# Thresholded spikes and a feed-forward table: another way to the idle row, other homes for sums, and another order of the loads

## The chip, the cores and the metric

One core of one Trainium2 chip. The metric is the device time of one execution of the kernel in microseconds (us); lower is better.

## The reference

`x` is (2, 2048, 512) float32, `cond` (2, 512), `w1` (512, 2048), `w2` (2048, 512). Cut to what matters:

```python
def _L0_cond_ref(inputs, initial_state):
    rates = jax.nn.relu(inputs) * DT                       # DT = 0.001
    c = initial_state[:, None, :] + jnp.cumsum(rates, axis=1)
    fl = jnp.floor(c)
    prev = jnp.concatenate([jnp.floor(initial_state)[:, None, :], fl[:, :-1, :]], axis=1)
    return (fl - prev) / DT

def _L0_ffn_ref(x, w1, b1, w2, b2):
    h = jax.nn.relu(jnp.einsum('bsd,dw->bsw', x, w1) + b1)
    return jnp.einsum('bsw,wd->bsd', h, w2) + b2

out = x + _L0_ffn_ref(_L0_cond_ref(x, cond), w1, b1, w2, b2)
```

Along the 2048 tokens each of the 2 x 512 channels passes a whole number very rarely, so nearly every row of spikes is zero. A token without a spike (an idle one) gets `x + relu(b1) @ w2 + b2`, the same row for all. A token with one spike in channel d gets the idle row and, on top, row d of a table `(relu(w1[d] / DT + b1) - relu(b1)) @ w2`. A token with more spikes goes through the network itself.

## The kernel before

All is float32. `x` is cut into 128 blocks of 16 tokens, a block to a partition, so that a batch is one tile `x_sb[b]` of 128 x 16 x 512. The inner width 2048 is cut into 16 chunks `m` of 128. Each engine has a list of work written out by hand, and semaphores tie the lists together.

**Loads** are issued by SyncE (SP) in one row (L272 to L297). `w_pairs` holds for each chunk the 128 rows of w1 transposed and of w2 side by side, 512 KB; a piece of `x` is two tokens of every block, 512 KB, eight to a batch (`load_x`). Pairs and pieces alternate. Then come `b2` and `w1` in four parts (L297, 4 MB in all, for the network's first layer), and last the stores of the finished idle rows (`store_idle`, L299), each behind a wait.

**ScalarE** makes each chunk of w1 into what the table needs by two steps, L422 and L423 (`table_chunk`), and copies the running sums out of PSUM (`copy_sums`, L427) behind chunks 6 and 11.

**TensorE** starts with eight products of ones (L900), and then multiplies chunk after chunk into four PSUM banks `ps_table` (L807): four products of 512 columns a chunk, each two records of the profile. Between the chunks stand small products that VectorE waits for or feeds (L901 to L931): `sum_totals(b)` makes block totals into running sums over blocks (L844), `spread_tokens(b)` writes the found tokens into all partitions (L856), `count_leads` (L862) and `find_slots` (L879) number the tokens with several spikes. Behind the table come the network's first layer (L888) and second layer (L895) for those tokens.

**VectorE** sums each batch over the 16 tokens of a block (`block_totals`, L547 to L552), so that `find_blocks` (L559 to L563) can tell in which block a channel passes its threshold; it then lists the blocks. **GpSimd** gathers the 16 values of each channel in its block (L342, four gathers a batch), and `find_tokens` (L582 to L588) finds the token in the block. `count_met` (L600), `find_leads`, `find_slots`, `first_spikes` and `second_spikes` prepare the rows of the network. Small levels and names are made early (`rise_levels`, `names`, L516 to L539).

**The idle row.** VectorE adds nine chunks of `relu(b1) * w2` into `idle_part` in SBUF (`idle_by_hand`, L509). TensorE adds the other seven and the part in four strips of 32 partitions (`add_strips`, L823 and L827), ScalarE copies them (L446), one product joins them (`join_strips`, L833), and ScalarE copies the row to SBUF (L448). It also stays in the bank `ps_idle`. Then it is added to all of `x_sb`: VectorE adds four tokens at once, with the row from PSUM (`add_idle`, L673, five times), GpSimd one token at once with the row from SBUF (L354, twelve times). GpSimd's additions wait for the semaphore `reading_psum` (L359 to L363), which VectorE raises ahead of steps of its own that read PSUM (L597, L706, L714).

At the end GpSimd adds the table's rows to the output by indirect DMAs (L347), behind the stores of the idle rows, and writes the rows of the network (L381).

Of the kernel before, what the change touches and what calls it, by code (L numbers as in the profile page):

```python
# [13 lines left out]
P = 128  # L14
# [4 lines left out]
def spike_ffn(nc, x, x_turned, cond, cond_cols, w1, w_pairs, b1_cols, b2, out):  # L19

# [14 lines left out]
    STRIP = 32  # L38
    STRIPS = P // STRIP
    BY_HAND = 9  # L40
# [14 lines left out]
    with ExitStack() as ctx:  # L55
# [6 lines left out]
        def psum(name):  # L62
            return ctx.enter_context(nc.psum_tensor(name, [P, 512], F32))

        x_sb = [sb(f"x_sb{b}", [P, BLK, D]) for b in range(B)]
        w_sb = sb("w_sb", [P, FC, 2, D])
        w1_sb = sb("w1_sb", [P, DC, F])
        total_two = [sb(f"total_two{b}", [P, TH, D]) for b in range(B)]
# [4 lines left out]
        idle_base = sb("idle_base", [P, D])  # L73
# [26 lines left out]
        strip_i = sb("strip_i", [P, 1], I32)  # L100
        strip_first = sb("strip_first", [P, 1])
# [38 lines left out]
        table_hidden = w_sb[:, :, 0, :]  # L140
        w2_sb = w_sb[:, :, 1, :]
        hidden = [w_sb[:, m // 4, 0, m % 4 * P:(m % 4 + 1) * P] for m in range(FC)]
        table_row = [w_sb[:, 4 + c, 0, :] for c in range(DC)]
        new_row = w_sb[:, 8, 0, :]
# [20 lines left out]
        ps_met = psum("ps_met")  # L165
        ps_small = psum("ps_small")
# [9 lines left out]
        w_in = [sem(f"w_in{m}") for m in range(FC)]  # L176
        w2_first_in = sem("w2_first_in")
# [4 lines left out]
        const_ready = sem("const_ready")  # L182
        ones_ready = sem("ones_ready")
# [33 lines left out]
        strip_first_ready = sem("strip_first_ready")  # L217
        strips_summed = sem("strips_summed")
        strips_copied = sem("strips_copied")
        idle_summed = sem("idle_summed")  # L220
        idle_copied = sem("idle_copied")
        reading_psum = sem("reading_psum")
# [32 lines left out]

        def redo_count(eng):

            return eng.value_load(redo_i[0:1, 0:1], min_val=1, max_val=BLK + 1)  # L258
# [4 lines left out]
        def _(sp):  # L263
            def load_pair(m):
                sp.dma_start(w_sb[:, m, :, :], w_pairs[m * P:(m + 1) * P, :, :]).then_inc(w_in[m], 16)
# [6 lines left out]
            sp.dma_start(w_sb[:, 0, 0, :], w_pairs[0:P, 0, :]).then_inc(w_in[0], 16)  # L272
            sp.dma_start(w_sb[:, 0, 1, :], w_pairs[0:P, 1, :]).then_inc(w2_first_in, 16)
            load_pair(1)
            sp.dma_start(start_c[:, :], cond_cols).then_inc(start_in, 16)
            load_x(0)
            load_pair(2)
            load_x(1)
            for m in range(3, 8):
# [713 lines left out]
```

## Time and profile before

| what | us |
|---|---|
| three runs | 104.23, 104.07, 102.87 |
| median | 104.07 |
| span of the profiled execution, first to last instruction | 102.1 |
| TensorE busy in it | 95.4 |
| VectorE | 65.9 |
| ScalarE | 35.5 |
| GpSimd | 43.2 |

The profile's page gives the span of the profiled execution and not its time with what lies around the span; the median of the runs is 1.97 above the span. Engines are named PE (TensorE), PEld (its weight loads), DVE (VectorE), ACT (ScalarE), POOL (GpSimd) and SP (SyncE) in the rows. L12 is line 12 of the kernel. A record of an engine's step gives its start from the span's begin and its length; in square brackets stands how long the engine sat idle before it, and what ended that.

### The profile page before, as it was taken

How to read it: one execution, taken by the hardware profiler on the slowest of the kernel's cores; microseconds unless marked ns; L12 is line 12 of the kernel's file. 1: busy time of each engine (PE TensorE's matmuls, PEld its weight loads, DVE VectorE, ACT ScalarE, POOL GpSimd, SP SyncE). 2: the span in 40 equal slices, each digit the busy share in tenths (PEclk: the TensorE clock that was granted, in tenths of full speed). 3: DMA queues.
4: the chain of work that ended last, by engine and by line, in shares of the span. 5: the costliest groups of instructions: out<-in, count | busy, mean ns of one | idle time of the engine just before them, and what ended most of it. 6: DMA issues, size and time to landing. Idle time of an engine off the chain costs nothing.

```text
span 102.1 us, 1157 instructions
## 1 busy us (share of the span) xinstructions
PE 95.4 (93%) x370; PEld 54.0 (53%) x370; DVE 65.9 (64%) x142; ACT 35.5 (35%) x64; POOL 43.2 (42%) x44
## 2 busy tenths in 40 slices
PE   5999999999999999999969999999999999999910
PEld 5944444444644444644234564649999984444300
DVE  2448999888699999488958888899993020020020
ACT  2796515315372540569740000003953330000000
POOL 6350000000078700017508181499937883688040
PEclk9999999999999999999999999999999999999996
DMA  1999999999999999999999725427999999998701
GB/s 58 286 387 414 417 420 411 411 407 409 409 409 409 396 393 401 409 394 387 379 373 352 324 116 218 193 125 292 395 430 436 407 336 195 218 115 106 92 8 62
DMA packets 10028, 31.66 MB, mean 310 GB/s; under 512 B 1671, under 2 KB 1799, under 8 KB 8994
## 3 DMA queue, kind: packets, MB, share of 16 engines
q1 hardware_dynamic: 8304, 29.63, 74.7%
q0 software_dynamic: 1568, 1.90, 11.4%
q8 instruction: 5, 0.08, 0.3%
q14 instruction: 5, 0.04, 0.1%
q10 hardware_dynamic: 146, 0.01, 0.1%
HBM read 21.58 MB, written 10.75 MB: 316 GB/s over the span
## 4 chain that ended last, share of the span: by engine, by line
PE 50%; DVE 20%; POOL 13%; issue 11%; ACT 1%; POOLq 1%; DVEq 0%
PE ps_table L807 40%; DVE x_sb L673 11%; POOL out L347 11%; PE ps_small L900 4%; DVE same L600 3%; PE ps_idle L823 2%; PE ps_turn L844 2%; DVE hot L619 1%; PE ps_idle L827 1%; PE ps_idle L833 1%; DVE spk_t L634 1%; POOL out L381 1%; POOL general_x L370 1%; POOLq L258 1%; DVE spk_t L629 1%
## 5 line engine op out<-in xcount | busy, mean ns | idle before, releaser
L807 PE MATMUL ps_table<-w_sb 128*128 128x512 f32 x128 | 56.9, 595 | 0.0
L807 PEld LDWEIGHTS ps_table<-w_sb 128*128 128x128 f32 x128 | 23.6, 190 | 27.1 <-issue 26.4
L342 POOL DMA_INDIRECT rates<-in_x_turned,sixteen_at x8 | 9.9, 1236 | 33.9 <-DVE sixteen_at L563 32.1
L354 POOL TENSOR_TENSOR x_sb<-x_sb,idle_row 128x512 f32<-128x512 f32 x12 | 14.9, 1277 | 9.9 <-DVEq L706 3.7
L422 ACT ACTIVATE w_sb<-w_sb,b_col 128x512 f32<-128x512 f32 (+2 forms) x19 | 12.2, 643 | 16.5 <-DMA w_sb<-in_w_pairs 16.3
L549 DVE SCALAR_TENSOR_TENSOR total_two<-x_sb,total_two 128x1024 f32<-128x1024 f32 x14 | 17.1, 1225 | 1.2 <-DMA x_sb<-in_x 0.8
L347 POOL DMA_INDIRECT out<-w_sb,to_single x8 | 12.5, 1558 | 5.8 <-issue 3.7
L895 PE MATMUL ps_table<-w_sb 128*128 128x512 f32 x32 | 14.0, 595 | 0.0
L423 ACT ACTIVATE w_sb<-w_sb,minus_relu_b 128x512 f32<-128x512 f32 (+2 forms) x19 | 12.3, 649 | 0.6
L673 DVE TENSOR_TENSOR x_sb<-x_sb,ps_idle 128x2048 f32<-128x2048 f32 x5 | 11.2, 2283 | 1.5 <-ACT idle_row L448 1.3
L895 PEld LDWEIGHTS ps_table<-w_sb 128*128 128x128 f32 x32 | 6.0, 190 | 7.2 <-issue 6.9
L452 ACT ACTIVATE w_sb<-ps_turn,b_col 128x128 f32<-128x128 f32 x8 | 2.9, 367 | 19.0 <-PE ps_turn L888 18.4
L888 PE MATMUL ps_small<-spk_t,w_sb 128*128 128x128 f32 x64 | 8.5, 275 | 0.0
L888 PE MATMUL ps_turn<-spk_t,w_sb 128*128 128x128 f32 x64 | 8.5, 275 | 0.0
L888 PEld LDWEIGHTS ps_turn<-spk_t,w_sb 128*128 128x128 f32 x64 | 7.9, 192 | 0.5 <-DVE spk_t L634 0.3
L888 PEld LDWEIGHTS ps_small<-spk_t,w_sb 128*128 128x128 f32 x64 | 7.8, 192 | 0.0
L509 DVE SCALAR_TENSOR_TENSOR idle_part<-w_sb,relu_b,idle_part 128x512 f32<-128x512 f32 x9 | 6.7, 750 | 1.5 <-DMA w_sb<-in_w_pairs 1.4
L729 DVE TENSOR_TENSOR w_sb<-ps_table,general_x 128x512 f32<-128x512 f32 x1 | 0.7, 692 | 6.3 <-PE ps_table L895 6.3
L900 PE MATMUL ps_small<-ones 128*128 128x128 f32 x16 | 3.7, 427 | 1.1 <-POOLq L320 1.1
L727 DVE TENSOR_TENSOR general_x<-general_x,b_row 128x512 f32<-128x512 f32 x1 | 0.7, 691 | 6.2 <-DMA general_x<-in_x,from_general 6.2
L900 PEld LDWEIGHTS ps_small<-ones 128*128 128x128 f32 x16 | 3.5, 330 | 1.1 <-POOLq L320 1.1
L665 DVE TENSOR_SCALAR crowd<-ps_table 128x1 f32<-128x1 f32 x1 | 0.2, 159 | 6.1 <-PE ps_table L871 6.1
(113 smaller groups left out, 65.5 us busy)
## 6 DMA issues: line engine op xcount, KB each, us to landing
x_sb<-in_x SPq DMA_DIRECT2D x16, 512.0 KB, 14.3
out<-x_sb SPq DMA_DIRECT2D x8, 1024.0 KB, 4.1
w_sb<-in_w_pairs SPq DMA_DIRECT2D x15, 512.0 KB, 15.7
w_sb<-in_w SPq DMA_DIRECT2D x4, 1024.0 KB, 15.3
w_sb<-in_w_pairs SPq DMA_DIRECT2D x2, 256.0 KB, 2.9
b_row<-in_b SPq DMA_DIRECT2D x1, 256.0 KB, 15.3
rates<-in_x_turned,sixteen_at POOLq DMA_INDIRECT x8, 6.5
out<-w_sb,to_single POOLq DMA_INDIRECT x8
```

The lines of the kernel that those rows point to most:

```text
L342: pool.indirect_dma_start(out=rates[:, col, :], out_offset=None, in_=x_sixteen, in_offset=bass.IndirectOffsetOnAxis(ap=sixteen_at[:, col:c ...
L347: pool.indirect_dma_start(out=out_rows, out_offset=bass.IndirectOffsetOnAxis(ap=to, axis=0), in_=row, in_offset=None, bounds_check=last_ro ...
L354: last = pool.tensor_tensor(x_sb[b][:, t, :], x_sb[b][:, t, :], idle_row[:, :], ALU.add)
L422: chain(act.activation(weights, weights, ACT.Relu, bias=b1_col[:, m:m + 1], scale=PER_DT))
L423: act.activation(weights, weights, ACT.Identity, bias=minus_relu_b1[:, m:m + 1]).then_inc(table_hidden_ready, 1)
L509: step = dve.scalar_tensor_tensor(out=idle_part[:, :], in0=w2_sb[:, m, :], scalar=relu_b1[:, m:m + 1], in1=idle_part[:, :], op0=ALU.mult, ...
L549: chain(dve.scalar_tensor_tensor(out=total_two[b][:, :, :], in0=tokens, scalar=0.0, in1=total_two[b][:, :, :], op0=ALU.max, op1=ALU.add))
L673: last = dve.tensor_tensor(tokens, tokens, along(ps_idle[:, :], end - begin), ALU.add)
L807: last = pe.matmul(ps_table[c][:, :], table_hidden[:, m, c * P:(c + 1) * P], w2_sb[:, m, :], start=(m == 0), stop=(m == FC - 1))
L888: last = pe.matmul(ps_hidden[m % 2][:, 0:P], w1_sb[:, c, m * P:(m + 1) * P], spk_t[:, c, :], start=(c == 0), stop=(c == DC - 1))
L895: last = pe.matmul(ps_out[:, :], hidden[m], w2_sb[:, m, :], start=(m == 0), stop=(m == FC - 1))
L900: pe.matmul(ps_small[:, 0:P], ones[:, :], ones[:, :], start=True, stop=True)
```

## The change

- The idle row: VectorE adds all 16 chunks, with the running sum in the PSUM bank `ps_idle` instead of SBUF; the last step writes `idle_part` in SBUF. TensorE sums it over the partitions by one product with ones (`sum_idle`) behind chunk 7. Strips, joining and their copy are gone.
- The block totals run in two PSUM banks (`ps_total`, which `ps_met` and `ps_small` are now parts of) instead of SBUF; the last step of a batch writes SBUF. The first of them waits for the products of ones.
- `rise_levels` and `names` move from VectorE to GpSimd, with `copy_predicated` written as products and sums.
- GpSimd's queue: gathers of batch 0, twelve tokens of the idle row, gathers of batch 1, eight more tokens. `reading_psum` is gone; instead each addition waits until VectorE has summed the piece. VectorE adds three quarters instead of five.
- `w_pairs` is split: w1's chunks in a layout of their own (2 KB a partition), w2 in eight groups of one to three chunks. The order of the loads is new; `w1` stands in between the first stores.
- Orders on VectorE and TensorE are new.

The core of the diff:

```diff
 @block.sync
+            load_w1_turned(0)
+            load_w2(0)
+            load_w1_turned(1)
+            load_w2(1)
+            sp.dma_start(start_c[:, :], cond_cols).then_inc(start_in, 16)
+            load_w2(2)
+            load_w1_turned(2)
+            load_x(0)
+            load_x(1)
+            load_w1_turned(3)
+            load_x(2)
+            load_x(3)
+            load_w2(3)
+            load_x(4)
+            load_w1_turned(4)
+            load_x(5)
+            load_x(6)
+            load_w1_turned(5)
+            load_x(7)
+            load_w2(4)
+            load_w2(5)
+            load_w1_turned(6)
+            load_w2(6)
+            load_w2(7)
+            load_x(8)
+            load_w1_turned(7)
+            for h in range(9, 11):
+                load_x(h)
+            load_w1_turned(8)
+            for h in range(11, 14):
+                load_x(h)
+            load_w1_turned(9)
+            load_x(14)
+            load_x(15)
+            for m in range(10, FC):
+                load_w1_turned(m)
+            sp.dma_start(b2_row[:, :], b2.rearrange("(o d) -> o d", o=1).to_broadcast([P, D])).then_inc(b2_in, 16)
+            store_idle(0, 0)
+            store_idle(0, 1)
+            load_w1(0)
+            load_w1(1)
+            store_idle(0, 2)
+            load_w1(2)
+            load_w1(3)
+            store_idle(0, 3)
+            for q in (0, 3, 1, 2):
+                store_idle(1, q)
...
+    W2_GROUPS = ((0, 1), (1, 2), (2, 4), (4, 6), (6, 9), (9, 12), (12, 14), (14, 16))
+        ps_total = psum("ps_total", TH)
+        ps_met = ps_total[:, 0:512]
+        ps_small = ps_total[:, 512:1024]
...
 @block.gpsimd
+            def rise_levels():
+                pool.wait_ge(goals_ready, 1)
+                pool.wait_ge(start_in, 16)
...
+            rise_levels()
+            names()
+            pool.sem_inc(levels_ready, 1)
...
                 for t in range(begin, end):
+                    pool.wait_ge(x_summed[b], t // TH + 1)
                     last = pool.tensor_tensor(x_sb[b][:, t, :], x_sb[b][:, t, :], idle_row[:, :], ALU.add)
...
+            get_sixteens(0)
             pool.wait_ge(idle_copied, 1)
-            pool.wait_ge(reading_psum, 1)
-            add_idle(0, 12, 14)
-            pool.wait_ge(reading_psum, 2)
-            add_idle(0, 14, 16)
-            pool.wait_ge(reading_psum, 3)
-            add_idle(1, 12, 16)
-            add_idle(1, 8, 12)
+            add_idle(0, 0, 12)
+            get_sixteens(1)
+            add_idle(0, 12, 16)
+            add_idle(1, 0, 4)
...
 @block.scalar
+                if m == 8:
+                    act.wait_ge(idle_summed, 1)
+                    act.activation(idle_row[:, :], ps_idle[:, :], ACT.Copy).then_inc(idle_copied, 1)
...
 @block.vector
+                step = dve.scalar_tensor_tensor(out=ps_idle[:, :] if m < FC - 1 else idle_part[:, :],
+                                                in0=w2_sb[:, m, :], scalar=relu_b1[:, m:m + 1],
+                                                in1=ps_idle[:, :] if m > 0 else idle_part[:, :], op0=ALU.mult, op1=ALU.add)
...
+                    if h == 0:
+                        step = dve.tensor_scalar(sums, tokens, 0.0, None, ALU.max)
+                    else:
+                        step = dve.scalar_tensor_tensor(out=sums if h < XH - 1 else total_two[:, :, :], in0=tokens, scalar=0.0,
+                                                        in1=sums, op0=ALU.max, op1=ALU.add)
+                    step.then_inc(x_summed[b], 1)
+                    dve.wait_ge(x_summed[b], h + 1)
...
             first_columns()
+            for m in range(4):
+                idle_by_hand(m)
+            block_totals(0, 0, 4)
+            idle_by_hand(4)
+            idle_by_hand(5)
+            block_totals(0, 4, XH)
+            for m in range(6, 12):
+                idle_by_hand(m)
             find_blocks(0)
+            for m in range(12, FC):
+                idle_by_hand(m)
+            block_totals(1, 0, 2)
             find_bases(0)
+            block_totals(1, 2, XH)
             find_blocks(1)
             find_tokens(0)
             find_bases(1)
             count_met(0)
             find_leads(0)
+            add_idle(1, 12, 16)
             find_tokens(1)
             find_slots(0)
             count_met(1)
             find_leads(1)
             first_spikes()
             find_slots(1)
             second_spikes()
             add_idle(1, 4, 8)
+            add_idle(1, 8, 12)
...
 @block.tensor
+            for m in range(6, 8):
                 table_chunk(m)
+            sum_idle()
+            for m in range(8, 10):
+                table_chunk(m)
+            table_part(10, 0, 2)
             sum_totals(1)
+            table_part(10, 2, DC)
+            table_part(11, 0, 3)
             spread_tokens(0)
+            table_part(11, 3, DC)
+            table_part(12, 0, 3)
             count_leads(0)
             table_part(12, 3, DC)
+            table_part(13, 0, 2)
             spread_tokens(1)
+            table_part(13, 2, DC)
             find_slots(0)
```

## Rows read from the trace of the kernel before

**Rows 1.** The page, part 1: busy us of each engine, share of span, instructions

```profile
PE 95.4 (93%) x370; PEld 54.0 (53%) x370; DVE 65.9 (64%) x142; ACT 35.5 (35%) x64; POOL 43.2 (42%) x44
```

**Rows 2.** Timeline of TensorE: start us, us, engine, line, operation, out<-in, count

```profile
1.11 3.71 PE L900 MATMUL ps_small<-ones 128*128 128x128 f32 x16 [1.11 <-POOLq L320]
4.66 20.79 PE L807 MATMUL ps_table<-w_sb 128*128 128x512 f32 x48
...
48.21 1.49 PE L823 MATMUL ps_idle<-w_sb,relu_b 128*32 128x512 f32 x11
...
52.95 1.88 PE L807 MATMUL ps_table<-w_sb 128*128 128x512 f32 x4
...
58.33 0.60 PE L856 MATMUL ps_turn<-ident,token 128*128 128x128 f32 x4
...
68.93 1.05 PE L888 MATMUL ps_turn<-spk_t,w_sb 128*128 128x128 f32 x8
...
83.36 13.98 PE L895 MATMUL ps_table<-w_sb 128*128 128x512 f32 x32
```

**Rows 3.** Groups of VectorE, shapes apart: busy us, mean ns of one, idle before

```profile
L549 DVE SCALAR_TENSOR_TENSOR total_two<-x_sb,total_two 128x1024 f32<-128x1024 f32 x14 | 17.1, 1225 | 1.2 <-DMA x_sb<-in_x 0.8
...
L509 DVE SCALAR_TENSOR_TENSOR idle_part<-w_sb,relu_b,idle_part 128x512 f32<-128x512 f32 x9 | 6.7, 750 | 1.5 <-DMA w_sb<-in_w_pairs 1.4
...
L600 DVE SCALAR_TENSOR_TENSOR same<-ps_met,token,weigh 128x512 bf16<-128x512 f32 x4 | 3.0, 751 | 0.1
...
L552 DVE TENSOR_TENSOR total<-total_two 128x512 f32<-128x512 f32 x2 | 1.4, 692 | 0.1
L559 DVE TENSOR_TENSOR under<-ps_turn,theta_sum 128x512 f32<-128x512 f32 x2 | 1.4, 692 | 2.3 <-PE ps_turn L844 2.3
...
L547 DVE TENSOR_SCALAR total_two<-x_sb 128x1024 f32<-128x1024 f32 x2 | 1.4, 690 | 0.4 <-DVE idle_part L509 0.4
```

**Rows 4.** Timeline of ScalarE: its steps on chunks 4, 6 and 11 as they land

```profile
15.59 0.72 ACT L422 ACTIVATE w_sb<-w_sb,b_col 128x512 f32<-128x512 f32 x1 [2.37 <-DMA w_sb<-in_w_pairs]
...
23.25 0.72 ACT L422 ACTIVATE w_sb<-w_sb,b_col 128x512 f32<-128x512 f32 x1 [2.35 <-DMA w_sb<-in_w_pairs]
24.01 0.72 ACT L423 ACTIVATE w_sb<-w_sb,minus_relu_b 128x512 f32<-128x512 f32 x1
...
41.04 0.72 ACT L422 ACTIVATE w_sb<-w_sb,b_col 128x512 f32<-128x512 f32 x1 [2.54 <-DMA w_sb<-in_w_pairs]
```

**Rows 5.** Timeline of VectorE

```profile
28.87 2.49 DVE L549 SCALAR_TENSOR_TENSOR total_two<-x_sb,total_two 128x1024 f32<-128x1024 f32 x2
...
41.26 0.69 DVE L552 TENSOR_TENSOR total<-total_two 128x512 f32<-128x512 f32 x1
...
56.10 0.42 DVE L582 TENSOR_SCALAR rates<-rates 128x64 f32<-128x64 f32 x1
...
65.15 2.29 DVE L673 TENSOR_TENSOR x_sb<-x_sb,ps_idle 128x2048 f32<-128x2048 f32 x1 [0.24 <-DVE hot L619]
```

**Rows 6.** Timeline of GpSimd: gathers of the rates, additions of the idle row

```profile
30.18 2.00 POOL L342 DMA_INDIRECT rates<-in_x_turned,sixteen_at  x1 [0.30 <-issue]
...
45.58 0.94 POOL L342 DMA_INDIRECT rates<-in_x_turned,sixteen_at  x1 [10.09 <-DVE sixteen_at L563]
...
53.96 2.51 POOL L354 TENSOR_TENSOR x_sb<-x_sb,idle_row 128x512 f32<-128x512 f32 x2 [3.69 <-DVEq L706]
...
65.14 9.93 POOL L354 TENSOR_TENSOR x_sb<-x_sb,idle_row 128x512 f32<-128x512 f32 x8 [3.44 <-DVEq L714]
```

**Rows 7.** The tile `rates`: ns min/median/max of a step, and the gathers' landing

```profile
L582 DVE TENSOR_SCALAR rates<-rates x2: 191/304/418, 45.2 to 56.1; 128x64 f32<-128x64 f32 x2
...
DMA to landing us min/median/max: 5.3/6.5/7.2
```

**Rows 8.** Windows: us, then each engine's busy us (instructions), clock, DMA share, GB/s

```profile
7.30:10.86 3.56, 3.56 (x10) 1.65 (x9) 2.98 (x19) 2.58 (x5) 0.00 (x0) 1.00 1.03 413
...
100.00:101.00 1.00, 0.00 (x0) 0.00 (x0) 0.00 (x0) 0.00 (x0) 0.00 (x0) 0.60 0.39 150
```

More of the change, by code:

```diff
@@ L16, with spike_ffn @@
 PER_DT = float(np.float32(1.0 / float(np.float32(DT))))
-def spike_ffn(nc, x, x_turned, cond, cond_cols, w1, w_pairs, b1_cols, b2, out):
+def spike_ffn(nc, x, x_turned, cond, cond_cols, w1, w1_turned, w2_rows, b1_cols, b2, out):
     B, S, D = x.shape
@@ L138, in spike_ffn @@
         redo_i = sb("redo_i", [P, 1], I32)
[L140 to L144, printed above, removed]
+        hidden = [table_hidden[:, m // 4, m % 4 * P:(m % 4 + 1) * P] for m in range(FC)]
+        table_row = [table_hidden[:, 4 + c, :] for c in range(DC)]
+        new_row = table_hidden[:, 8, :]
         again = x_sb[0]
@@ L175, in spike_ffn @@
         x_in = [[sem(f"x_in{b}_{h}") for h in range(XH)] for b in range(B)]
-        w_in = [sem(f"w_in{m}") for m in range(FC)]
-        w2_first_in = sem("w2_first_in")
+        w1_turned_in = [sem(f"w1_turned_in{m}") for m in range(FC)]
+        w2_in = [sem(f"w2_in{g}") for g in range(len(W2_GROUPS))]
         w1_in = [sem(f"w1_in{i}") for i in range(WQ)]
@@ L182, in spike_ffn @@
         const_ready = sem("const_ready")
+        goals_ready = sem("goals_ready")
+        levels_ready = sem("levels_ready")
+        warm_ended = sem("warm_ended")
+        x_summed = [sem(f"x_summed{b}") for b in range(B)]
         ones_ready = sem("ones_ready")
@@ L254, in own @@
             return slice(b * DC, (b + 1) * DC)
+        w2_group = [g for g, (begin, end) in enumerate(W2_GROUPS) for _ in range(begin, end)]
         def redo_count(eng):
@@ L336, in _, with names, get_sixteens @@
+            def names():
+                pool.wait_ge(const_ready, 3)
+                chain(pool.tensor_copy(slot_name[:, :], slot_i[:, :]))
+                chain(pool.tensor_copy(sixteen_f[:, :], sixteen_i[:, :]))
+            rise_levels()
+            names()
+            pool.sem_inc(levels_ready, 1)
             last_row = pool.to_reg(ROWS - 1)
-            for b in range(B):
+            def get_sixteens(b):
                 pool.wait_ge(sixteen_listed, b + 1)
@@ L899, in _ @@
             for _ in range(WARM):
-                pe.matmul(ps_small[:, 0:P], ones[:, :], ones[:, :], start=True, stop=True)
+                last = pe.matmul(ps_small[:, 0:P], ones[:, :], ones[:, :], start=True, stop=True)
+            last.then_inc(warm_ended, 1)
             for c in range(DC):
```

186 lines of the change are left out of this document (46 added, 140 removed).

## Prediction

> **What bounds the kernel now.** I read the page first: TensorE is busy in 95.4 of 102.1 us [rows 1]. Then TensorE's timeline, which shows the end being set by that row of work: eight products of ones from 1.1, the table from 4.7 in records of 0.43 us (20.79 us for 48; a product of two records is 0.86, a chunk of four products 3.44), the first layer from 68.93, the second layer to 97.34, and hardly a gap [rows 2]. One stretch of it is not table work: from 48.21 to 52.95 stand the idle row's strips and their joining, and one table product that the program puts between them (L917). Everything after 68.93 is 28.4 us of TensorE and then a fixed tail of 4.8, and the change leaves both alone. So the question is one date: when does the first layer start? It needs all of the table ahead of it on TensorE's queue, and in that queue stand nine waits on results of VectorE (two of totals, the idle part, two spreads, two counts of leads, two of slots). So I read next what feeds those waits: VectorE's groups [rows 3], ScalarE's dates for the chunks' arrival [rows 4], VectorE's timeline [rows 5], GpSimd's timeline and its gathers' landing [rows 6, 7], and two windows [rows 8].
>
> The page gives the execution's span, 102.1; the median of the three runs is 104.07, so some 2.0 us lie around the span. I add changes of the span to the median.
>
> **TensorE's own work.** Removed: 52.95 - 48.21 = 4.74, less the table product in it, 0.86: 3.9 us [rows 2]. Added: one product of 512 columns, 0.86. Net -3.0, if nothing waits. This is the gain on offer.
>
> **Loads.** Count the SP queue in units of 256 KB. Before, chunk 4's pair is unit 18 and ScalarE starts on it at 15.59 the moment it lands; chunk 6's is unit 30, at 23.25; chunk 11's unit 56, at 41.04 [rows 4]. That is 0.64 us a unit, and 1.1 us more behind GpSimd's first gathers. ScalarE takes two steps of 0.72 with small gaps, 1.5 us, from landing to ready [rows 4]. After: w1's chunk 4 is unit 21 (lands 17.5, ready 19.0), chunk 6 unit 35 (26.5, 28.0), chunk 7 unit 42 (31.0, 32.5), chunk 9 unit 54 (39.6, 41.1). TensorE wants them at 4.8 + 3.44 a chunk and 0.9 for the first totals: chunk 4 at 18.6, so it waits 0.4; chunk 6 at 26.8, waits 1.2; chunk 7 at 31.4, waits 1.0; the idle product ends at 36.8; chunk 9 wanted at 40.2, waits 0.9. Sum 3.5 us, which is the gain given back. That w1 now comes in rows of 2 KB (pairs were 4 KB) no row prices apart; I take nothing, with 0 to 1 us by unit 54.
>
> **VectorE to the second totals.** It loses 3.5 us of small levels and names, 18 operations that fill the window from 7.30 to 10.86 [rows 8], and gains seven additions of 0.79 (0.75 and the gap, rows 3), 5.5 us. The first operation of each batch now writes PSUM. Its row is 0.69 for 1024 elements while the two-input form of the same size takes 1.23 [rows 3]; I take 1.23, since the fast rate is seen only between SBUF tiles, with 0.69 as the other bound (1.1 us for two). Other PSUM operands cost nothing: an addition from PSUM is 0.692 and one in SBUF 0.692 [rows 3]. The Trainium skill, VectorE: DVE Perf Modes, section on the TRN2 errata, gives an operation from PSUM 62 cycles of 0.96 GHz more than one from SBUF, some 0.06 us; an estimate by it is 2 us more over about 30 operations. By that page the second totals would be later still, but the two equal rows speak against it, and it stays out of the sum.
> Dates: x's eighth piece is unit 28, lands 22.0; totals end at 23.95, as before. Six idle additions to 28.65, the block search 1.7 (two steps of 0.69 like those of rows 3, a short one, gaps) to 30.3, four more to 33.4, two totals to 35.9, the bases 1.9 (two of 0.69, three short ones) to 37.8, six totals of 1.26 and the sum 0.69 to 46.1. Before it was 41.95 [rows 5]: 4.1 later, and VectorE, not the loads, sets it.
> Moved levels on GpSimd: some 25 chained small operations from 6.5. Between 0.3 and 0.9 us each they end at 14 to 29; they are wanted at 28.65. At 0.4 they are hidden.
>
> **GpSimd's queue, the step that decides.** Gathers of batch 0: with VectorE reading one SBUF tile only, four at 1.25 a piece, 30.6 to 35.6. Idle row copied at 36.9 + 0.6 = 37.5. Then twelve additions of 1.24 (9.93 for eight, rows 6) to 52.4, and only behind them the gathers of batch 1, which before were issued from 45.6 on. The last of four starts 3.75 us after the first, and lands 5.3 to 7.2 us after its issue [rows 7], I take 6: at best 52.4 + 3.75 + 6 = 62.2. Before, VectorE started on that batch's tokens at 56.10, held only by other work [rows 5].
>
> **What the two engines do to each other.** GpSimd's second gather takes 2.00 us instead of 0.94: it starts at 30.18 while VectorE adds two SBUF tiles until 31.36, and is 1.06 longer [rows 5, 6]. The other way: VectorE's rates step, 0.19 the other time, takes 0.42 from 56.10 [rows 5, 7] and ends at 56.52, right behind the end of GpSimd's additions at 56.47 [rows 6]. In no row does VectorE use two SBUF tiles while a further addition of GpSimd is queued; the steps beside GpSimd's eight additions from 65.14 read PSUM and keep their length. So the price of one such meeting lies between 0 and the rest of GpSimd's addition, 1.24. I take that rest, since both meetings that the trace has last to the end of the other's work. The Trainium skill, SBUF — State Buffer, section on who interferes with whom, calls the pair of interfaces that the two engines share an exclusive lock held for a whole instruction, which a VectorE instruction with one SBUF input doesn't need. By that rule the change is right to put its totals into PSUM and wrong to let the additions run beside the short steps between SBUF tiles: it gives rival A below, and its absence rival B.
> Short steps that now fall beside GpSimd's additions: the last of the bases at 37.7 (+1.2), the second total (+0.6, half an addition on average): totals at 47.9 instead of 46.1, so TensorE, which is there at 46.3 (chunk 9 from 41.1, then two products of chunk 10), waits 1.8. Then the second block search (+0.6), and three steps of batch 0's tokens until GpSimd is through, at about 54.1: token date 55.5 against TensorE's 53.3, wait 2.3. Bases 1.9, four counts of 0.8 [rows 3] and leads 0.6 end at 61.2: wait 1.8 at the first count of leads. VectorE adds its first quarter of the idle row, 2.3 [rows 5], to 63.5; the gathers, issued from 54.1, have landed at 63.9. GpSimd has begun eight more additions at 59.1, and ends them at about 70.2 with VectorE's steps between. Five steps of batch 1's tokens meet them, each 0.2 to 0.3 long and, but for the first, behind a whole addition: 63.9 + 0.6 + 4 x 1.45 makes 70.3, which is where the additions end, so 70.3 for the tokens. TensorE has been waiting since 63.9: 6.4 us.
> Behind that date TensorE has 11.4 us to the first layer: before, 10.6 from 58.33 [rows 2], and one table product more stands behind the spread now. VectorE's chain beside it, from the rates step to the last spikes, needs at most 68.93 - 56.10 less the idle addition of 2.3 that no longer stands in it [rows 2, 5], 10.5; it is covered. First layer at 81.7.
>
> **The clock.** TensorE's last product ends at 97.34 and it idles from there; the microsecond from 100 to 101 has a mean granted clock of 0.60, on the way from 2.4 GHz to the lower level of 1.2 [rows 8]. The first sixteen records ran at 0.23 us where equal ones at full rate take 0.11 [rows 2], so the stretch at the lower level cost 3.71 / 2 = 1.9 us. I take it that a wait of 6.4 us brings such a stretch once; bounds 0 and twice that. First layer at 83.5.
>
> **Sum.** 83.5 - 68.93 = +14.5; 104.07 + 14.5 = 118.5. GpSimd's rows to the output need about 20 us from the list at 87 and end before 107, while TensorE ends at 112: hidden, with 5 us of cover. w1, behind the early stores, is issued by 55 and lands by 65: wanted at 82, hidden by TensorE's wait.
>
> **Rivals.**
> *A, above*, 118.5, its own range 114.5 to 122. Chance 0.55.
> *B, late gathers alone.* VectorE's short steps are not held by GpSimd's additions, or hardly. Then tokens at 62.2 + 1.7 = 63.9, first layer at 75.3, and with the clock's 1.9 at 77.2: +8.3, 112.4; without the clock 110.5. For it: only one row shows a held VectorE step. 0.28.
> *C, GpSimd's additions hold the tile ports for the whole series.* They overlap (1.24 apart, 1.27 long, rows 6), so VectorE might not get in between. The bases' last step would wait from 37.7 to 52.4, and the second totals, 7.6 us of work, come at 60.8, which puts all behind it 6 us or more later than in A: 124 or more. Against it: GpSimd got in between VectorE's back-to-back steps at 31.36. 0.11.
> *D, the other side.* The early additions are short enough that batch 1's gathers are not late. It decides at VectorE's second block list, about 47.5: twelve additions in the 10.0 us from 37.5, 0.83 each where rows 6 show 1.24. Then TensorE's -3.0 stands. With the waits for loads as counted (3.5) it is 104.6; if the loads land some 1.2 us sooner than counted, which takes all four waits, it is 101.1. 0.06, half of it faster.
> The change may also not do what it says: were the totals in PSUM to hold GpSimd all the same, its additions get longer, which is A with a worse number.
>
> **How the numbers follow.** Predicted is A's 118.5. The range goes from B with no clock loss, 110.5, to A's upper end, 122.5; it leaves out C, D and the low edge of B, some 0.2. Faster by over 2% (what a measurement here can tell): 0.03; within 2%: 0.03; slower by over 2%: A, B, C, 0.94.
>
> **What would show it.** Right: TensorE's chain with waits for chunks 4, 6, 7 and 9 of 0.4 to 1.2 us; second totals 4 to 6 us later than 41.95; gathers of batch 1 issued from 52 to 55; the token steps beside GpSimd's additions at 1.2 to 1.5 us instead of 0.2; one wait of TensorE of 5 to 7 us ahead of the second spread, and a granted clock of half behind it; the first layer from 81 to 85. Wrong: token steps at their old 0.2 us (B), one VectorE step of over 5 us (C), the first layer ahead of 70 (D); and if the first operation into PSUM stays at 0.69, that term goes. The prediction fails as a whole if GpSimd's additions run well below 1.24 us.

## The result, and the profile after

Four executions of the changed kernel took 120.27 to 121.46 us, median 120.93, beside 104.15 for the kernel before on the same chip (102.87 to 104.32). The ratio is 1.166, with an interval of 1.157 to 1.175: slower by a sixth. 118.5 was predicted, with a range of 110.5 to 122.5. Ratios and times leave disturbed executions out (two of four of the first experiment, its profiled one among them, and one of four of the second).

The page of the profiled execution (120.95 us, span 119.1), its first part and the row of the granted clock in 40 slices:

```profile
PE 98.1 (82%) x354; PEld 54.7 (46%) x354; DVE 76.7 (64%) x129; ACT 34.8 (29%) x63; POOL 57.5 (48%) x77
...
PEclk9999999999999999999965555999999999999999
```

TensorE has 16 records fewer than in [rows 1] and is busy for 2.7 us longer: the stretch at 5 tenths of the clock adds some 3 us of busy time to work that got shorter, and the rest lies in short waits that the records cover. Where it stands still is in its timeline (start, length, line, count, and in brackets the idle time before and what ended it):

```profile
26.08 1.05 PE L842 MATMUL ps_turn<-up_to,total 128*128 128x128 f32 x8
28.07 3.70 PE L822 MATMUL ps_table<-w_sb,table_hidden 128*128 128x512 f32 x8 [0.93 <-ACT table_hidden L472]
32.58 3.70 PE L822 MATMUL ps_table<-w_sb,table_hidden 128*128 128x512 f32 x8 [0.82 <-ACT table_hidden L472]
36.12 1.02 PE L832 MATMUL ps_idle<-idle_part,ones 128*128 128x512 f32 x2
...
41.07 5.42 PE L822 MATMUL ps_table<-w_sb,table_hidden 128*128 128x512 f32 x12 [0.50 <-ACT table_hidden L472]
47.12 1.16 PE L842 MATMUL ps_turn<-up_to,total 128*128 128x128 f32 x8 [0.63 <-DVE total L582]
...
54.11 0.65 PE L854 MATMUL ps_total<-ident,token 128*128 128x128 f32 x4 [1.54 <-DVEq L621]
54.60 3.60 PE L822 MATMUL ps_table<-w_sb,table_hidden 128*128 128x512 f32 x8
68.69 0.59 PE L860 MATMUL ps_total<-leads_run,upper 128*128 128x1 f32 x2 [10.49 <-DVEq L641]
69.14 5.42 PE L822 MATMUL ps_table<-w_sb,table_hidden 128*128 128x512 f32 x6
74.40 0.60 PE L854 MATMUL ps_turn<-ident,token 128*128 128x128 f32 x4
...
85.65 1.05 PE L886 MATMUL ps_turn<-spk_t,w_sb 128*128 128x128 f32 x8
```

The strips are gone (one product at 36.12 in their place), five waits of 0.50 to 1.54 us have come in, and then one of 10.49 us ahead of the first count of leads. Behind it six records take 5.42 us where eight took 3.60 ahead of it. The first layer starts at 85.65 instead of 68.93 [rows 2]; from there to the second layer it is 14.4 us as before. So the whole loss, 16.7 us, again lies ahead of the first layer, and the longest wait is on VectorE. Its timeline there:

```profile
45.43 1.64 DVE L582 TENSOR_TENSOR total<-total_two 128x512 f32<-128x512 f32 x1
...
50.59 0.18 DVE L613 TENSOR_SCALAR rates<-rates 128x64 f32<-128x64 f32 x1
50.81 1.25 DVE L614 TENSOR_TENSOR_SCAN climb<-token_keep,rates 128x64 f32<-128x64 bf16 x1
52.09 1.13 DVE L616 TENSOR_TENSOR climb<-climb,sum_at 128x64 f32<-128x64 f32 x1
...
59.35 8.83 DVE L636 SCALAR_TENSOR_TENSOR is_first<-met,valid 128x4 f32<-128x4 f32 x1 [0.15 <-DVE same L629]
...
70.93 0.19 DVE L613 TENSOR_SCALAR rates<-rates 128x64 f32<-128x64 f32 x1
71.15 0.29 DVE L614 TENSOR_TENSOR_SCAN climb<-token_keep,rates 128x64 f32<-128x64 bf16 x1
71.48 0.23 DVE L616 TENSOR_TENSOR climb<-climb,sum_at 128x64 f32<-128x64 f32 x1
```

And GpSimd's:

```profile
37.86 15.28 POOL L405 TENSOR_TENSOR x_sb<-x_sb,idle_row 128x512 f32<-128x512 f32 x12 [2.12 <-ACT idle_row L494]
53.29 0.96 POOL L392 DMA_INDIRECT rates<-in_x_turned,sixteen_at  x1 [0.15 <-issue]
...
58.38 9.78 POOL L405 TENSOR_TENSOR x_sb<-x_sb,idle_row 128x512 f32<-128x512 f32 x8
```

Read the two together. Beside the first series (37.86 to 53.14) the steps of VectorE that take two SBUF tiles wait for the rest of an addition: 1.64 instead of 0.69, 0.73 instead of 0.16 (the list of blocks at 49.94), 1.25 instead of 0.29, 1.13 instead of 0.23. The step at 50.59, with one SBUF tile, keeps its 0.18 here; in other kernels such a step was held as well (last section). Beside the second series (58.38 to 68.16) a step over 4 columns, 0.16 us when free, takes 8.83 and ends 0.02 us behind the last addition: it was held not by one addition but by all that were left. The tokens of batch 1 then run at their free length.

The granted clock, in windows of one microsecond (us, busy time and instructions of the five engines, clock, DMA share, GB/s):

```profile
60.00:61.00 1.00, 0.00 (x0) 0.00 (x0) 1.00 (x1) 0.00 (x0) 1.00 (x2) 0.87 0.96 396
61.00:62.00 1.00, 0.00 (x0) 0.00 (x0) 1.00 (x1) 0.00 (x0) 1.00 (x1) 0.50 1.01 390
73.00:74.00 1.00, 1.00 (x2) 0.26 (x2) 0.52 (x1) 0.00 (x0) 0.00 (x0) 0.50 0.97 393
74.00:75.00 1.00, 1.00 (x6) 0.60 (x5) 0.00 (x0) 0.00 (x0) 0.00 (x0) 0.81 0.32 131
```

TensorE ran dry at about 58.2; in the microsecond from 60 the clock begins to leave 2.4 GHz, from 61 it is at 1.2, and it comes back within 74 to 75, more than 5 us after work was there again at 68.69.

### The profile page after: what moved, and what is told of

Same layout as the page of the kernel before. It is cut to its first block, busy times and chain, and to the rows that moved or that the text cites. A ratio compares the mean times of both kernels' runs of the same rounds, so it can differ in the third digit from the quotient of the medians.

```text
span 119.1 us, 1179 instructions
## 1 busy us (share of the span) xinstructions
PE 98.1 (82%) x354; PEld 54.7 (46%) x354; DVE 76.7 (64%) x129; ACT 34.8 (29%) x63; POOL 57.5 (48%) x77
## 4 chain that ended last, share of the span: by engine, by line
DVE 36%; PE 18%; issue 13%; POOL 11%; DMA 11%; SPq 7%; POOLq 1%; ACT 1%; DVEq 0%
PE ps_table L822 12%; DMA x_sb<-in_x 11%; POOL out L397 10%; DVE is_first L636 7%; DVE ps_total L577 6%; DVE ps_idle L558 6%; SPq L271 3%; DVE same L629 3%; SPq L258 2%; DVE total_two L577 2%; DVE total L582 2%; PE ps_turn L886 2%; PE ps_total L877 1%; SPq L262 1%; DVE under L602 1%
## 5 line engine op out<-in xcount | busy, mean ns | idle before, releaser
L822 PE MATMUL ps_table<-w_sb,table_hidden 128*128 128x512 f32 x128 | 60.8, 625 | 2.2 <-ACT table_hidden L472 2.2
L822 PEld LDWEIGHTS ps_table<-w_sb,table_hidden 128*128 128x128 f32 x128 | 24.5, 200 | 31.1 <-issue 24.7
L405 POOL TENSOR_TENSOR x_sb<-x_sb,idle_row 128x512 f32<-128x512 f32 x20 | 25.1, 1289 | 2.1 <-ACT idle_row L494 2.1
L397 POOL DMA_INDIRECT out<-table_hidden,to_single x8 | 12.5, 1559 | 23.5 <-ACT table_hidden L506 21.7
L471 ACT ACTIVATE table_hidden<-table_hidden,b_col 128x512 f32<-128x512 f32 (+2 forms) x19 | 12.2, 642 | 18.6 <-DMA table_hidden<-in_w_turned 18.6
L577 DVE SCALAR_TENSOR_TENSOR ps_total<-x_sb,ps_total 128x1024 f32<-128x1024 f32 x12 | 14.8, 1229 | 1.5 <-DMA x_sb<-in_x 1.1
L893 PE MATMUL ps_table<-w_sb,table_hidden 128*128 128x512 f32 x32 | 14.0, 595 | 0.0
L472 ACT ACTIVATE table_hidden<-table_hidden,minus_relu_b 128x512 f32<-128x512 f32 (+2 forms) x19 | 12.3, 649 | 0.6
L558 DVE SCALAR_TENSOR_TENSOR ps_idle<-w_sb,relu_b,ps_idle 128x512 f32<-128x512 f32 x14 | 10.6, 754 | 2.3 <-DMA w_sb<-in_w_rows 2.0
L893 PEld LDWEIGHTS ps_table<-w_sb,table_hidden 128*128 128x128 f32 x32 | 6.0, 190 | 7.2 <-issue 6.9
L636 DVE SCALAR_TENSOR_TENSOR is_first<-met,valid 128x4 f32<-128x4 f32 x2 | 9.0, 4496 | 0.3 <-DVE same L629 0.3
L886 PE MATMUL ps_total<-spk_t,w_sb 128*128 128x128 f32 x64 | 8.5, 275 | 0.0
## 6 DMA issues: line engine op xcount, KB each, us to landing
w_sb<-in_w_rows SPq DMA_DIRECT2D x2, 768.0 KB, 14.6
```

Source lines behind the costliest of these rows:

```text
L397: pool.indirect_dma_start(out=out_rows, out_offset=bass.IndirectOffsetOnAxis(ap=to, axis=0), in_=row, in_offset=None, bounds_check=last_ro ...
L405: last = pool.tensor_tensor(x_sb[b][:, t, :], x_sb[b][:, t, :], idle_row[:, :], ALU.add)
L471: chain(act.activation(weights, weights, ACT.Relu, bias=b1_col[:, m:m + 1], scale=PER_DT))
L472: act.activation(weights, weights, ACT.Identity, bias=minus_relu_b1[:, m:m + 1]).then_inc(table_hidden_ready, 1)
L558: step = dve.scalar_tensor_tensor(out=ps_idle[:, :] if m < FC - 1 else idle_part[:, :], in0=w2_sb[:, m, :], scalar=relu_b1[:, m:m + 1], in ...
L577: step = dve.scalar_tensor_tensor(out=sums if h < XH - 1 else total_two[:, :, :], in0=tokens, scalar=0.0, in1=sums, op0=ALU.max, op1=ALU.add)
```

## Experiments

Ratios are against the kernel before, run on the same chip. Eight kernels were run.

### The second series apart from the short steps, in two ways

What is open is why one step lasted 8.83 us, and what the time would be without it. The first kernel keeps GpSimd's second series back until the last spikes are made; the second lets it run at once, but puts a small step ahead of it that GpSimd waits for.

```diff
             get_sixteens(1)
+            pool.wait_ge(spikes_made, 1)
             add_idle(0, 12, 16)
...
             second_spikes()
+            dve.sem_inc(spikes_made, 1)
```

> The changed kernel with GpSimd's second series of eight additions held back until VectorE has made the last spikes; gathers and first series as they are. Theory S (VectorE's step between two SBUF tiles is held by the whole second series, 8.83 us, and TensorE's clock falls in that wait): the first leads come at about 60 instead of 68.6, the gathers of batch 1 land near 63.5 and then set the tokens at 65, the first layer starts at 76 to 78 instead of 85.65, no stretch at the half clock, and the time is 111 to 113 us. Theory N (the late gathers alone set the date, and the held step is hidden behind them): 120 to 121 us, no change.

```diff
             get_sixteens(1)
+            chain(pool.memset(joint[:, :], 0.0))
             add_idle(0, 12, 16)
```

> The changed kernel with one small memset on GpSimd, waited for to its end, between the gathers of batch 1 and the second series of eight additions. Theory K (the series holds its tile ports throughout because it follows the gathers without a wait, with GpSimd's cores out of step, so that no moment between two additions is free on all of them): VectorE's step of 8.83 us falls to at most 1.3, its later steps between SBUF tiles take 0.7 to 1.3 each while the series runs, and the time falls by 2 to 6 us, to 115 to 119. Theory L (whether a step gets in between two additions has nothing to do with what stands ahead of the series): the step stays at 8 to 9 us and the time at 120 to 121.

Held back: ratio 1.096 [1.088, 1.104], some 113.8 us, just above the 111 to 113 that were expected. Every VectorE step between the gathers and the held-back series has its free length (the scan 0.29, the addition behind it 0.23), and the step that took 8.83 takes 0.16. Its profiled execution differs from the expectation in two ways. The first layer starts at 78.60, not 76 to 78, and there is a stretch at the lower clock after all, of some 3.4 us, that begins in the microsecond from 66. Besides, the end is GpSimd's: its rows of batch 1 wait 7.22 us for a store of the idle rows, and the last row follows them without a gap at 109.53, while its value was ready at 107.81. So 113.8 us is not the price of the late gathers alone.

With the waited step: ratio 1.116 [1.109, 1.123], 116.0 us, inside what was expected. The series is as long as before, and the step over 4 columns has fallen from 8.83 us to 0.46. VectorE in this kernel:

```profile
59.86 0.46 DVE L638 SCALAR_TENSOR_TENSOR is_first<-met,valid 128x4 f32<-128x4 f32 x1 [0.15 <-DVE same L631]
60.36 1.18 DVE L640 SCALAR_TENSOR_TENSOR leads<-met,is_first 128x4 f32<-128x4 f32 x1
61.57 1.19 DVE L642 TENSOR_TENSOR_SCAN leads_run<-ones,leads 128x4 f32<-128x4 f32 x1
62.91 2.29 DVE L704 TENSOR_TENSOR x_sb<-x_sb,ps_idle 128x2048 f32<-128x2048 f32 x1
65.11 0.19 DVE L615 TENSOR_SCALAR rates<-rates 128x64 f32<-128x64 f32 x1
65.34 1.24 DVE L616 TENSOR_TENSOR_SCAN climb<-token_keep,rates 128x64 f32<-128x64 bf16 x1
66.61 1.13 DVE L618 TENSOR_TENSOR climb<-climb,sum_at 128x64 f32<-128x64 f32 x1
67.77 1.19 DVE L619 TENSOR_TENSOR under<-climb,theta 128x64 f32<-128x64 f32 x1
```

Behind the first, which meets only the rest of an addition, each step with two SBUF tiles lasts about one addition, 1.13 to 1.24. This is what the prediction had taken for both series.

### The same small step, not waited for

The waited step changes two things: there is an instruction between gathers and additions, and GpSimd stands still for a moment. The control leaves out the second.

```diff
             get_sixteens(1)
+            pool.memset(joint[:, :], 0.0)
             add_idle(0, 12, 16)
```

> Control for the joined kernel: the same small memset between the gathers and the second series, but nothing waits for it. Theory K (what frees the ports between additions is that all of GpSimd's cores start the series together): without the wait VectorE's step is again held for the whole series, 7 to 9 us, and the time is 119.5 to 122. Theory T (the memset only shifted the moment at which VectorE's step comes): the step stays at 0.5 to 1.3 us and the time at 115.5 to 117, as joined.

Ratio 1.167 [1.161, 1.172], the changed kernel's own. VectorE:

```profile
59.31 8.85 DVE L638 SCALAR_TENSOR_TENSOR is_first<-met,valid 128x4 f32<-128x4 f32 x1 [0.15 <-DVE same L631]
```

So the wait makes the difference and not the instruction. Nor is it the moment at which the step comes: it met the series 0.97, 0.96 and (totals in SBUF, below) 1.59 us behind its start where it was held throughout, and 0.82 us behind it where it was not. That a series started straight behind gathers keeps a VectorE step with two SBUF tiles out for its whole rest, and one started from a wait for one addition at a time, is shown; that GpSimd's cores run out of step in the first case is my picture of it, and no run here looks into it. Price: 120.9 - 116.0 = 4.9 us.

### GpSimd's additions let loose in the kernel before

```diff
             pool.wait_ge(idle_copied, 1)
-            pool.wait_ge(reading_psum, 1)
             add_idle(0, 12, 14)
-            pool.wait_ge(reading_psum, 2)
             add_idle(0, 14, 16)
-            pool.wait_ge(reading_psum, 3)
             add_idle(1, 12, 16)
```

> The kernel before, with the three waits of GpSimd's additions for VectorE's PSUM steps taken out: twelve additions in one series from about 53.8, as soon as the idle row is copied, with nothing else of the change. Theory S and K: the series starts behind a wait, so VectorE gets in between additions, each of its steps between SBUF tiles costs up to 1.25 us more until about 69, batch 1's tokens come 3 to 5 us later, and the time rises by 4 to 9 us, to 108 to 113. Theory L (a series can hold a step throughout at any time): one VectorE step of 6 us or more and a rise of over 9 us. Theory H (harmless, only the change's queue order matters): 103 to 105 us.

Ratio 1.058 [1.051, 1.065], 109.8 us, inside what was expected. The gathers are issued within 0.7 us of their dates before, nothing else is changed, and VectorE's steps show the price beside twelve additions that start from a wait:

```profile
55.72 0.28 DVE L579 TENSOR_SCALAR rates<-rates 128x64 f32<-128x64 f32 x1
56.03 1.29 DVE L580 TENSOR_TENSOR_SCAN climb<-token_keep,rates 128x64 f32<-128x64 bf16 x1
57.35 1.12 DVE L582 TENSOR_TENSOR climb<-climb,sum_at 128x64 f32<-128x64 f32 x1
...
62.10 1.72 DVE L616 TENSOR_TENSOR hot<-slot,slot_name 128x512 f32<-128x512 f32 x1
```

The first layer moves from 68.93 to 74.88. The three waits on `reading_psum`, which look like a loss of GpSimd's time, are worth 6 us.

### The totals back in SBUF

```diff
-    step = dve.tensor_scalar(sums, tokens, 0.0, None, ALU.max)
+    step = dve.tensor_scalar(total_two[:, :, :], tokens, 0.0, None, ALU.max)
...
-    step = dve.scalar_tensor_tensor(out=sums if h < XH - 1 else total_two[:, :, :], in0=tokens, scalar=0.0,
-                                    in1=sums, op0=ALU.max, op1=ALU.add)
+    step = dve.scalar_tensor_tensor(out=total_two[:, :, :], in0=tokens, scalar=0.0,
+                                    in1=total_two[:, :, :], op0=ALU.max, op1=ALU.add)
```

> The changed kernel with the block totals back in SBUF (both their first operations at 0.69 us instead of 1.23, so 1.1 us less of VectorE), everything else as changed. Theory S (two SBUF tiles collide with GpSimd's additions, PSUM totals don't): from about 37 on each of the last totals waits for an addition and each addition for a total; the second totals come at 51 to 54 instead of 47.1, GpSimd's first series ends at 58 to 62 instead of 53.1, and the time rises to 124 to 131 us. Theory P (the totals' home is worth nothing): 119 to 121, second totals 1 us earlier.

Ratio 1.214 [1.208, 1.220], 125.6 us, inside what was expected: the change's PSUM totals do what they are for. VectorE and, in the second fence, GpSimd:

```profile
37.44 12.26 DVE L577 SCALAR_TENSOR_TENSOR total_two<-x_sb,total_two 128x1024 f32<-128x1024 f32 x6
...
65.12 8.21 DVE L636 SCALAR_TENSOR_TENSOR is_first<-met,valid 128x4 f32<-128x4 f32 x1 [0.15 <-DVE same L629]
```

```profile
37.98 20.67 POOL L405 TENSOR_TENSOR x_sb<-x_sb,idle_row 128x512 f32<-128x512 f32 x12 [1.66 <-ACT idle_row L494]
```

Six operations take 2.04 us each instead of 1.23, and twelve additions 1.72 each instead of 1.27. With the totals in PSUM the same six take 6.29 (five) and 1.22 us, and only the joining step at the end (0.69 free, 1.64 here) is held.

### Gathers ahead of the additions, the second series kept back

```diff
             pool.wait_ge(idle_copied, 1)
-            add_idle(0, 0, 12)
+            add_idle(0, 0, 8)
             get_sixteens(1)
-            add_idle(0, 12, 16)
-            add_idle(1, 0, 4)
+            pool.wait_ge(spikes_made, 1)
+            add_idle(0, 8, 16)
...
             store_idle(0, 0)
             store_idle(0, 1)
             load_w1(0)
             load_w1(1)
-            store_idle(0, 2)
             load_w1(2)
             load_w1(3)
+            store_idle(0, 2)
...
             second_spikes()
+            dve.sem_inc(spikes_made, 1)
             add_idle(1, 4, 8)
+            add_idle(1, 0, 4)
```

> The changed kernel with only eight of GpSimd's additions ahead of the gathers of batch 1, the other eight of batch 0 behind VectorE's last spikes, and batch 1's first quarter added by VectorE; w1's last two parts are loaded ahead of the store of batch 0's third quarter. Theory S with late gathers: without the held step the gathers are the next limit (gate alone: 111 to 113), and 3.5 us earlier gathers bring the tokens to about 61.5, the first layer to 73 to 74.5 and the time to 108 to 110, where GpSimd's rows to the output begin to set the end. Theory G (behind the held step stands something other than the gathers, VectorE's own list or the loads): no more than 1 us below the gated kernel.

The first layer starts at 73.36, as expected, with no wait of TensorE above 1.2 us and no stretch at the lower clock. Even so it is 4.4 us later than before: in this trace the waits for chunks (4.2), second totals (0.9), leads (1.3) and tokens (1.1) outweigh the 3.0 saved. And the time is 112.5 (ratio 1.085 [1.079, 1.092]), above the expected 108 to 110: the end is no longer TensorE's. GpSimd at the end:

```profile
98.28 1.57 POOL L398 DMA_INDIRECT out<-table_hidden,to_single  x1 [3.97 <-DMA out<-x_sb]
...
105.69 1.03 POOL L431 DMA_INDIRECT out<-table_hidden,to_general  x1 [0.31 <-issue]
```

With the additions kept back until 71, the stores of the idle rows come late, the rows of batch 1 wait 3.97 us for them, and the last row follows them without a gap, while its value was ready at 102.6. So here the miss is that of the end, as in the kernel with the second series alone held back: I had priced GpSimd's queue only up to the first layer.

### Parts of the change on the kernel before

Levels and names on GpSimd, totals and idle sum in PSUM, 13 chunks and one round of strips instead of two, the second totals one product earlier on TensorE; everything else as before. The part of the diff that places the additions:

```diff
-    BY_HAND = 9
+    BY_HAND = 13
...
             find_bases(0)
             block_totals(1, 5, 6)
             idle_by_hand(8)
+            idle_by_hand(9)
+            idle_by_hand(10)
             block_totals(1, 6, XH)
+            idle_by_hand(11)
             find_blocks(1)
             find_tokens(0)
+            idle_by_hand(12)
```

> The kernel before with the parts of the change that cost nothing by the runs so far: levels on GpSimd, totals and the idle sum in PSUM, and with the freed time 13 chunks of the idle row by VectorE instead of nine, so four strips on TensorE instead of eight; the second totals one table product earlier; loads, GpSimd's queue and its waits for VectorE's PSUM steps as before. If TensorE's row sets the end and VectorE keeps up: 1 to 2 us below the kernel before, a ratio of 0.98 to 0.99. If VectorE's chain behind the gathers of batch 1 sets it (they land at 55 to 56 whatever the strips do): a ratio of 0.995 to 1.005. Over 1.01: the additions by hand have moved VectorE's chain late.

Ratio 1.019 [1.015, 1.023]: slower, though by how far it is from 2% can't be told; it is the third of the three expectations. TensorE, where the second totals are wanted:

```profile
43.93 1.16 PE L869 MATMUL ps_turn<-up_to,total 128*128 128x128 f32 x8 [1.76 <-DVE total L572]
```

The second totals end at 43.87 instead of 41.95: two additions more (1.6 us) and a first operation into PSUM (+0.54) stand ahead of them, with 0.24 of waiting for a load used up. And the 3.5 us that VectorE saved early bring nothing: batch 0's totals end at 24.2 here, 24.0 before and 24.1 in the changed kernel, because the landing of `x` sets them in all three.

The other try leaves levels and totals as they were, and puts the four additions more into waits that VectorE has:

```diff
-            find_blocks(0)
             idle_by_hand(6)
+            find_blocks(0)
...
-            block_totals(1, 6, XH)
+            block_totals(1, 6, 7)
+            idle_by_hand(9)
+            block_totals(1, 7, XH)
+            idle_by_hand(10)
+            idle_by_hand(11)
             find_blocks(1)
             find_tokens(0)
+            idle_by_hand(12)
...
-            add_idle(0, 4, 8)
             second_spikes()
+            add_idle(0, 4, 8)
...
-            table_part(12, 0, 1)
+            table_part(12, 0, 2)
             join_strips()
```

(and two more table products ahead of the second spread).

> The kernel before with one idea of the change (more of the idle row by hand) and new places for it. VectorE adds 13 chunks: the 7th stands in its wait ahead of the first block search, the 10th ahead of the last piece's totals, two in the 1.63 us wait behind the second totals, the last behind the tokens of batch 0. TensorE's strips then need one round of four instead of two (-0.9 us), two table products stand ahead of the joining instead of one (its wait of 0.8 us goes), two more ahead of the second spread, and VectorE's addition of 2.3 us moves from ahead of the last spikes to behind them. If TensorE's row and VectorE's chain behind the second spread bound the kernel before together, as its trace reads, both get shorter by some 1.5 us: first layer at 67.2 to 68.0 instead of 68.93, 102.4 to 103.2 us, ratio 0.983 to 0.992. If the additions by hand cost what they did in the kernel with levels on GpSimd, where the second totals came 1.9 us late, the ratio is 1.00 to 1.02.

Ratio 1.011 [1.007, 1.016]: no gain, and slightly slower, the second of the two expectations. TensorE does save 1.6 us, but the first layer starts at 68.78 against 68.93. The second totals came at 43.43, 1.5 later than before, behind a wait of 0.77 for a piece of `x` that the trace of before doesn't have at that place, and the second tokens at 58.78 instead of 57.81. At the end GpSimd waits 4.14 us for a store of the idle rows, instead of 2.06 (probably the moved addition made it later), and has 0.6 us left ahead of the last row instead of 3.8:

```profile
90.56 1.56 POOL L347 DMA_INDIRECT out<-w_sb,to_single  x1 [4.14 <-DMA out<-x_sb]
...
98.27 1.03 POOL L381 DMA_INDIRECT out<-w_sb,to_general  x1 [0.60 <-DVE w_sb L734]
```

The last row is issued 0.15 us earlier than before and lands 3.5 us later instead of 2.7, which makes up the 0.7 us by which this span is longer (102.8 to 102.1); why it lands later, no run shows. No version here beats the kernel before, where GpSimd has only those 3.8 us to spare ahead of the last row.

## Why the prediction was right, and where its steps were off

The sum by steps of TensorE, from start to start, so that filling and emptying count with the wait. "Due" is the start before plus 0.86 a product, 0.89 a totals step and 0.43 a spread (41.07 + 6 x 0.86 = 46.23, and so on; 24 products from 4.67 give 25.31):

| step | predicted | measured |
|---|---|---|
| strips gone, one product instead | -3.0 | -3.0 |
| chunks 4, 6, 7, 9 | 3.5 | 0.8 (26.08, due 25.31) + 1.1 + 1.1 + 0.6 = 3.6 |
| second totals | 1.8 | 47.12, due 46.23: 0.9 |
| first spread | 2.3 | 54.11, due 52.31: 1.8 |
| first count of leads | 1.8 | 68.69, due 57.98: 10.7 |
| second spread | 6.4 | 0 |
| clock | 1.9 | 74.40, due 71.41: 3.0 |
| first layer (by dates; the parts are rounded, and small waits of the kernel before, 0.3 in all, are not in them) | +14.5 | +16.7 |

**Loads.** ScalarE started on the chunks at these dates (its timeline), against 17.5, 26.5, 31.0 and 39.6 predicted:

```profile
17.58 0.72 ACT L471 ACTIVATE table_hidden<-table_hidden,b_col 128x512 f32<-128x512 f32 x1 [4.31 <-DMA table_hidden<-in_w_turned]
...
26.54 0.72 ACT L471 ACTIVATE table_hidden<-table_hidden,b_col 128x512 f32<-128x512 f32 x1 [4.25 <-DMA table_hidden<-in_w_turned]
...
31.06 0.72 ACT L471 ACTIVATE table_hidden<-table_hidden,b_col 128x512 f32<-128x512 f32 x1 [0.92 <-DMA table_hidden<-in_w_turned]
...
37.18 0.60 ACT L494 ACTIVATE idle_row<-ps_idle 128x512 f32<-128x512 f32 x1 [1.42 <-PE ps_idle L832]
39.54 0.72 ACT L471 ACTIVATE table_hidden<-table_hidden,b_col 128x512 f32<-128x512 f32 x1 [1.77 <-DMA table_hidden<-in_w_turned]
```

Counting the queue in units of 256 KB gave every date to 0.1 us, and the new order of the loads gave back by itself what the missing strips had gained. The rows of 2 KB cost nothing that can be seen.

**VectorE's additions.** The first operation into PSUM took 1.23, and operands in PSUM nothing more: the idle additions 754 ns against 750 in SBUF, the totals 1229 against 1225 [rows 3], so the 0.06 us that the prediction named and left out of its sum doesn't show. The idle row was copied by 37.8 (37.5 predicted). The levels were done on GpSimd by 14.6, the lower end of what was given for them, and hidden.

**GpSimd's queue.** Additions of 1.27, gathers of batch 1 issued from 53.29 (52.4 predicted).

**The two engines on one another.** The rule taken, a meeting costs the rest of one addition, held in the first series, and in both series of the three kernels whose second series starts behind a wait. The step that failed is this one: "Five steps of batch 1's tokens meet them, each 0.2 to 0.3 long and, but for the first, behind a whole addition." They met none. Even in the kernel with the waited step, where VectorE gets in between, three steps of these tokens were held and not five. The series held the leads of batch 0 throughout, from 59.35 to 68.18: rival C's mechanism, in the second series only, where C had placed it in the first. It is also the prediction's own sign of being wrong, "one VectorE step of over 5 us (C)"; and TensorE's long wait stood ahead of the count of leads, not of the second spread. Two slips are in the same paragraph. I let the leads end at 61.2 undisturbed though additions had begun at 59.1; the kernel with the waited step shows its three steps at 0.46, 1.18 and 1.19 instead of 0.16, 0.16 and 0.17. And I charged the second totals 1.8 (its own dates, 46.3 and 47.9, give 1.6) where TensorE waited 0.9: the bases ended before the additions began, so only one of the two meetings came about. Forecast A in its pure form is the kernel with the waited step, and it takes 116.0, not 118.5; the hold of the whole series adds 4.9. The predicted time is close by luck: a mechanism that A did not have made up for terms that were sized too high.

By the Trainium skill, SBUF — State Buffer, section on who interferes with whom, whichever of the two instructions comes first has the shared interfaces for its whole length and the other blocks. The prediction took from it that a VectorE instruction with one SBUF input doesn't need them; the page says so only outside the two-port modes, and which mode the one-tile steps that were held ran in (last section) no run shows. The first series agrees with the whole-instruction lock (1.13 to 1.25 a step); the second does not, with 8.83 us over the rest of eight instructions, and there the measurement decides.

**Clock.** One stretch at the lower level, as predicted, but it cost 3.0 and not 1.9 us: I took the length from the start of the kernel, 3.7 us, and here 5.7 us passed between the first product behind the wait and the one at full rate.

**Rivals.** B, late gathers alone: 112.4 was given for a kernel without holds. The one whose second series is kept back has late gathers and held steps in the first series alone, and takes 113.8, but its end is GpSimd's; no run here is B in its pure form. D: the additions did not get shorter.

**The end.** GpSimd's rows were hidden, as said: it waited 9.67 us ahead of the last row. In the kernels where TensorE came earlier that cover was gone.

## What to carry to other kernels

Before giving GpSimd a long series of two-tile operations, list VectorE's short steps with two SBUF tiles that fall beside it: each can cost up to a whole operation of GpSimd, whatever its own size, and an operand in PSUM (or a gate like `reading_psum`) kept them free here. Don't count on a step with one SBUF tile being free. If the series follows indirect DMAs on the same queue, try a waited step between; here it was worth 4.9 us. And count a reordered load queue in bytes: it gave the dates to 0.1 us here, and shows an engine's early relief to be worth nothing where loads set its pace.

## What was not expected of the hardware

- Eight additions of GpSimd, started directly behind an indirect DMA on its queue, held one VectorE step of 0.16 us for 8.83, 8.85 and 8.21 us in three kernels, until the last of them; behind a waited memset of 0.11 us the same step took 0.46.
- Steps with one SBUF tile behaved both ways. A TENSOR_SCALAR of 64 elements between SBUF tiles, 0.19 us when free, took 0.18 to 0.28 us beside running additions in five kernels, but 1.33 with the totals in SBUF; one of 8 elements, 0.17 when free, took 1.20 in both kernels with a held-back series. What decides it, no run here shows. The 0.42 in [rows 5], one of the two rows from which I had priced the meetings, is such a step. From the kernel with the totals in SBUF, and from that with the gathers ahead:

```profile
56.14 1.33 DVE L613 TENSOR_SCALAR rates<-rates 128x64 f32<-128x64 f32 x1
```

```profile
79.83 1.20 DVE L654 TENSOR_SCALAR not_single<-single 128x8 f32<-128x8 f32 x1
```

- TensorE's lower clock lasted 5.7 us from the restart. In the kernel with the waited step TensorE waited only 4.17 us, from 58.7 to 62.9, and the clock was at its lower level from 61 until between 67 and 68. Its windows:

```profile
61.00:62.00 1.00, 0.00 (x0) 0.00 (x0) 0.97 (x2) 0.00 (x0) 1.00 (x2) 0.50 0.93 366
...
67.00:68.00 1.00, 1.00 (x3) 0.21 (x1) 0.97 (x2) 0.00 (x0) 1.00 (x2) 0.59 1.07 442
```
